# First 38 expert tiles of an attention-and-experts kernel as 19 pairs with standing weights

## The chip, the cores and the metric

The kernel runs on one core of a Trainium2 chip. The metric is the device time of one execution in microseconds (us); lower is better.

## The reference

A batch of 32 sequences of 112 tokens with 256 channels (x) and a context of 375 rows of 192 channels. Cut to what is computed:

```python
x = x + xattn(layernorm(x), ctx)          # 16 heads of 64, softmax over 375 keys, projection 1024 -> 256
h = layernorm(x)
p = softmax(h @ gate_w); take the best 2 of 8 experts, shares normalised to 1
gate, up = split(h @ gate_up_w[e])        # 256 -> 2 * 512
y_e = (silu(gate) * up) @ down_w[e]       # 512 -> 256
x = x + sum over the 2 experts of share * y_e
```

3584 tokens with two experts each make 7168 rows of expert work, in float32.

## The kernel before

**Stages.** First the attention, two batches to an iteration, up to about 1130 us. While it runs, each token's normalised row h, with its token number and share behind it (258 floats), is scattered twice into `bins`, an HBM buffer with one region for each expert. Then the experts' stage: rows are taken from the bins in tiles of 128 rows of one expert. There are always NT = 63 tiles. The first N1 = 45 are whole tiles that can be planned before the last two batches are in the bins; the plan for the rest (`tiles_left`, `experts_left`, `rows_left` on VectorE) is worked out beside the first tiles, along with the last two batches' routing. `tile_row` and `tile_expert` hold each tile's place and expert; engines read them into registers.

**Precision.** Each float32 product is made of three matmuls on a high and a low part of both operands (`split_product`: high x high, high x low, low x high). ScalarE writes high parts by a copy, VectorE low parts by a subtraction. All experts' gate and up weights stand in SBUF as both parts (`Wgu`, 4 KB a row), the down weights (`Wd`) whole, for all 8 experts; the parts of one tile's down weights are made anew for each tile in `down_even` / `down_odd`.

**A tile t.** SyncE (`load_rows`, L595) loads 128 rows into one of four slots of `h_in`. TensorE turns them (`turn_rows`, L1678, 2 transposes); ScalarE (L963) and VectorE (L1347) make `hT_h`, `hT_l`; VectorE keeps token numbers and shares (`keep_dest`, L1355, L1356). TensorE's gate and up products (`hidden`, L1692) have the 128 rows as standing weights and 512 expert columns moving: 6 matmuls of 512 columns each. ScalarE applies silu (L992), VectorE multiplies (L1390) into `silu` [128 rows, 512]. That lies the wrong way round for the down product, so TensorE turns it (L1729, 4 transposes), ScalarE and VectorE make `hidT_h` (L987) and `hidT_l` (L1382). The down product has 12 matmuls of 256 columns. ScalarE scales by the share (L1008, `y_out`, `y_done`); GpSimd adds the rows into `out` in HBM by an indirect accumulating transfer (L822, semaphores `y_store`). An addition is issued only when the one before it has landed, since two tiles may hold the same token.

**Order.** Each engine runs its own stream written by hand in `four_tiles` (three iterations unrolled, then a loop of 4 tiles). TensorE's order in iteration t is: turn rows of t+1, turn hidden of t-1, up product of t, gate product of t+1, down product of t-1. ScalarE's: rows' high part of t+1, hidden high part of t-1, silu of t, down weights' high part of t (L1000), output of t-1. VectorE's: rows' low part, hidden low part of t-1, `keep_dest` of t+1, multiply of t, down weights' low part of t (L1392). SyncE only loads rows, up to 3 tiles ahead. All matmuls of `split_product` stand under L1429, row transposes under L1682. Before the stage, experts' gate and up weights are loaded by SyncE and ScalarE (L443), split by ScalarE (L857) and VectorE (L1138), and `Wd` by two SyncE transfers of 1024 and 3072 KB during the last attention batches.

## Time and profile before

| | us |
|---|---|
| median of 3 runs | 1472.36 (1471.12 to 1476.83) |
| the profiled execution | 1469.35 |
| its span, first to last instruction | 1467.6 |
| TensorE busy | 1426.4 (97%) |
| VectorE / ScalarE / GpSimd busy | 1054.7 / 854.5 / 624.9 |
| mean granted TensorE clock | 0.994 |

All times inside the kernel are us from the start of that span. A releaser, as in "<-PE bank L1429", is the instruction whose semaphore ended a wait. TensorE's matmuls overlap in the records: the pace of a stream is read from the starts, not from the durations.

### The profile page before, as it was taken

How to read it: one execution, taken by the hardware profiler on the slowest of the kernel's cores; microseconds unless marked ns; L12 is line 12 of the kernel's file. 1: busy time of each engine (PE TensorE's matmuls, PEld its weight loads, DVE VectorE, ACT ScalarE, POOL GpSimd, SP SyncE). 2: the span in 40 equal slices, each digit the busy share in tenths (PEclk: the TensorE clock that was granted, in tenths of full speed). 3: DMA queues.
4: the chain of work that ended last, by engine and by line, in shares of the span. 5: the costliest groups of instructions: out<-in, count | busy, mean ns of one | idle time of the engine just before them, and what ended most of it. 6: DMA issues, size and time to landing. Idle time of an engine off the chain costs nothing.

```text
span 1467.6 us, 38599 instructions
## 1 busy us (share of the span) xinstructions
PE 1426.4 (97%) x11960; PEld 1264.4 (86%) x11961; DVE 1054.7 (72%) x2868; ACT 854.5 (58%) x2392; POOL 624.9 (43%) x671
## 2 busy tenths in 40 slices
PE   6999999999999999999999999999997999999996
PEld 5888889888888888888888898888886788888885
DVE  5667777777777777777777777777767776666664
ACT  5566556555665566656655656566555565555553
POOL 3634344344545343544344444545436243333332
PEclk9999999999999999999999999999999999999999
DMA  9322222222222232322222222212128243333232
GB/s 264 108 68 69 75 72 76 67 76 67 73 67 75 72 88 76 99 74 67 73 67 77 70 73 70 73 38 73 31 64 312 50 69 54 57 51 57 51 57 26
DMA packets 101508, 114.75 MB, mean 78 GB/s; under 512 B 17276, under 2 KB 88172, under 8 KB 101356
## 3 DMA queue, kind: packets, MB, share of 16 engines
q1 hardware_dynamic: 88300, 95.25, 22.3%
q0 software_dynamic: 12144, 15.66, 6.0%
q10 hardware_dynamic: 1024, 3.34, 0.7%
q8 instruction: 21, 0.34, 0.1%
q14 instruction: 19, 0.16, 0.0%
HBM read 62.28 MB, written 51.93 MB: 78 GB/s over the span
## 4 chain that ended last, share of the span: by engine, by line
PE 91%; DVE 3%; DMA 3%; issue 1%; ACT 0%; ACTq 0%; POOLq 0%; DVEq 0%; SPq 0%
PE bank L1486 26%; PE bank L1429 21%; PE bank L1555 11%; PE bank L1531 10%; PE bank L1521 9%; PE bank L1576 6%; PE bank L1493 4%; DMA out<-y_out,dest_now 2%; PE bank L1729 2%; DVE probT L1285 1%; PE bank L1682 1%; DVE Wgu L1138 1%; DMA WkU_whole<-in_L_xattn_Wkv 1%; DVE stat L1127 0%; DVE x L1125 0%
## 5 line engine op out<-in xcount | busy, mean ns | idle before, releaser
L891 ACT ACTIVATE prob<-bank,neg_max 112x375 f32<-112x375 f32 x512 | 300.4, 589 | 136.1 <-DVE neg_max L1279 136.1
L1279 DVE TENSOR_REDUCE neg_max<-bank 112x1 f32<-112x375 f32 x512 | 243.8, 539 | 16.4 <-PE bank L1521 16.3
L1531 PE MATMUL bank<-ident,prob 112*125 112x112 f32 x1536 | 213.8, 273 | 2.6 <-ACT prob L891 2.4
L1531 PEld LDWEIGHTS bank<-ident,prob 112*125 112x125 f32 x1536 | 198.3, 188 | 16.1 <-ACT prob L891 4.7
L1555 PEld LDWEIGHTS bank<-probT,V 125*64 125x64 f32 x3072 | 149.0, 137 | 39.7 <-issue 37.0
L822 POOL DMA_INDIRECT out<-y_out,dest_now x63 | 97.8, 1552 | 199.9 <-DMA out<-y_out,dest_now 139.8
L1046 DVE TENSOR_TENSOR K_l<-bank,K_h 128x376 fp32r<-128x376 f32 x256 | 140.3, 549 | 57.1 <-ACT K_h L847 52.7
L1555 PE MATMUL bank<-probT,V 125*64 125x112 f32 x3072 | 176.6, 264 | 3.3 <-DVE probT L1285 2.5
L1429 PE MATMUL bank<-Wgu,hT_h 128*128 x504 | 164.7, 408 | 3.4 <-DVE hT_l L1347 2.8
L845 ACT COPY V<-bank 125x512 f32<-125x512 f32 x96 | 56.4, 587 | 164.7 <-PE bank L1493 162.2
L847 ACT CAST K_h<-bank 128x376 fp32r<-128x376 f32 x256 | 121.0, 473 | 31.2 <-PE bank L1486 29.7
L745 POOL TENSOR_SCALAR std<-mv 112x1 f32<-112x1 f32 x32 | 7.7, 239 | 280.2 <-DVE mv L1132 280.2
L710 POOL CAST OT_h<-O_now 128x448 fp32r<-128x448 f32 x64 | 37.3, 583 | 210.0 <-DVE O_now L1115 210.0
L897 ACT COPY probT<-bank 125x336 f32<-125x336 f32 x256 | 101.7, 442 | 38.6 <-PE bank L1531 37.8
L1285 DVE COPY probT<-bank 125x336 f32<-125x336 f32 x256 | 123.8, 494 | 0.1
L1036 DVE COPY V<-bank 125x512 f32<-125x512 f32 x96 | 66.4, 691 | 78.1 <-PE bank L1493 75.1
L1486 PE MATMUL bank<-yA_h,WkH 128*128 128x376 f32 x256 | 99.6, 389 | 13.1 <-DVE WkU L1064 13.1
L1008 ACT ACTIVATE y_out<-bank,share_now 128x256 f32<-128x256 f32 x63 | 29.8, 474 | 137.5 <-PE bank L1429 137.5
L1429 PEld LDWEIGHTS bank<-Wgu,hT_h 128*128 128x128 f32 x504 | 89.7, 189 | 23.2 <-issue 6.6
L891 ACT ACTIVATION_READ_ACCUMULATOR prob<-bank,neg_max 112x1 f32 x512 | 108.3, 212 | 0.0
L1429 PE MATMUL bank<-Wgu,hT_l 128*128 x252 | 99.2, 394 | 0.0
L1486 PE MATMUL bank<-WvH,yA_h 128*125 128x512 f32 x192 | 91.0, 474 | 0.0
(217 smaller groups left out, 3962.1 us busy)
## 6 DMA issues: line engine op xcount, KB each, us to landing
bins<-pad_rows SPq DMA_DIRECT2D x29, 1032.0 KB, 6.0
inv_rows<-sums SPq DMA_DIRECT2D x126, 128.0 KB, 2.9
h_in<-bins SPq DMA_DIRECT2D x63, 129.0 KB, 2.2
Wgu<-in_L_ffn_gate_up_w SPq DMA_DIRECT2D x6, 1024.0 KB, 6.8
y_sb<-in_ctx SPq DMA_DIRECT2D x32, 187.5 KB, 2.7
y_sb<-in_ctx SPq DMA_DIRECT2D x62, 93.8 KB, 2.7
x_sb<-in_x SPq DMA_DIRECT2D x16, 224.0 KB, 2.9
x_res<-in_x SPq DMA_DIRECT2D x32, 112.0 KB, 2.5
```

The source lines that it names most:

```text
L822: pool.indirect_dma_start(out, bass.IndirectOffsetOnAxis(ap=dest_now[:, (k + 3) % 4:(k + 3) % 4 + 1], axis=0), y_out[:, (k + 1) % 2, :], N ...
L847: nc.scalar.copy(K_h[:, arg, :], src[:, 0:LKE]).then_inc(hi_done, 1)
L891: nc.scalar.activation(prob[:, j, :], S_ps[j][0:LQ, 0:LKV], ACT.Exp, bias=neg_max[:, j:j + 1], accum_out=row_sum[:, head // HB, head % HB: ...
L897: nc.scalar.copy(probT[:, j, :], S_ps[j][0:KR, 0:KT * LQ]).then_inc(probT_second, 1)
L1046: nc.vector.tensor_tensor(lo, ps, hi.bitcast(F32), ALU.subtract).then_inc(lo_done, 1)
L1279: nc.vector.tensor_reduce(neg_max[:, j:j + 1], S_ps[j][0:LQ, 0:LKV], AX.X, ALU.max, negate=True).then_inc(max_done, 1)
L1285: nc.vector.tensor_copy(probT[:, j, :], S_ps[j][0:KR, 0:KT * LQ]).then_inc(probT_first, 1)
L1429: last = mm(dst, w, m, start=n == 0, stop=n == len(todo) - 1)
L1486: last = mm(out, w, y, start=begins and n == 0, stop=ends and n == "both")
L1521: last = mm(S_ps[2 * k + r][0:LQ, 0:LKE], w[rows, p, q], m[rows, p, :], start=n == 0, stop=n == len(todo) - 1)
L1531: last = nc.tensor.transpose(S_ps[j][0:KR, t * LQ:t * LQ + LQ], prob[:, j, t * KR:t * KR + KR], ident[0:LQ, 0:LQ])
L1555: last = mm(O_ps[r * DK:r * DK + DK, c:c + LQ], V[:, t, (2 * p + r) * DK:(2 * p + r) * DK + DK], probT[:, 2 * k + r, t * LQ:t * LQ + LQ], ...
```

## The change

- The first 38 tiles (N1 = 2 x 19) are planned as 19 pairs of one expert (PAIRS): 256 rows. 25 tiles remain single (before: 45 and 18).
- In a pair, 128 x 128 blocks of the expert's gate and up weights are the standing operand and the 256 turned rows move (`turned_hidden`): 12 matmuls of 256 columns for gate and as many for up, for each of two halves of the 512 hidden columns. The hidden values come out turned, and the pair has no transposes of them.
- These weights are held in `still`, one buffer for each half of gate and up, refilled for every pair: the high part by a copy on ScalarE (`hold_still`, 128 x 512 elements, four a pair), the low part by a transfer from `Wgu` to `still` inside SBUF (256 KB, four a pair, issued by SyncE, each behind the wait for the product that read the buffer last). The first pair's first half comes with both parts by transfer.
- `still` takes the place of most of `Wd`. `Wd` now has 2 slots; a pair's or single tile's down weights (512 KB) are loaded from HBM by SyncE (`load_down`, semaphores `wd_in`), two pairs or two tiles ahead. ScalarE waits for them in `hi_of_down`.
- In single tiles SyncE first waits for the addition of tile t-1, then loads rows of t+4 and down weights of t+2. The product of silu and up is written into `in_fours`, every fourth hidden column together, so that the down weights can be read with 4 KB in a piece.
- GpSimd issues a pair's two additions without a wait between them; before the first it waits for both of the pair before.
- The unrolled last-batch work and the plan move to pairs 0 to 7. The plan has one step more.
- TensorE's order in an iteration of pair p: down product of p-1, turn rows of p+1, gate and up of p's second half, gate and up of p+1's first half.

The core of the diff:

```diff
-N1 = -(-(2 * LQ * (B - 2) - E * (P - 1)) // P)
+PAIRS = -(-(2 * LQ * (B - 2) - E * (2 * P - 1)) // (2 * P))
+N1 = 2 * PAIRS
...
+def over_tiles(eng, pair_of_tiles, tile, end=PAIRS // 2, last=NT // 4):
+    for i in range(4):
+        for m in range(2):
+            pair_of_tiles(i, m)
+    with eng.Fori(4, end) as i:
+        for m in range(2):
+            pair_of_tiles(i, m)
...
+    pair_of_tiles(PAIRS // 2, 0)
+    for k in (2, 3):
+        tile(PAIRS // 2, k)
+    with eng.Fori(PAIRS // 2 + 1, last) as i:
+        for k in range(4):
+            tile(i, k)
...
+        place["at"] = wd_at
+        Wd = sb("Wd", [P, 2, FJ, C], F32)
+        still_at = place["at"]
...
+        in_fours = nc.alloc_sbuf_tensor_at("in_fours", [P, FJ, P], F32, offset=still_at)
...
+        still = sb("still", [P, 2, 2, 2, 2, 2 * P], F32R)
+        down_parts = [down_even, sb("down_odd", [P, 2, FJ, C], F32R)]
...
-                    sp.dma_start(Wd[:, 0:early].rearrange("p e k n -> p (e k) n"),
...
-                        sp.dma_start(Wd[:, early:E].rearrange("p e k n -> p (e k) n"),
...
+            def load_down(e, slot, rows="(k p)"):
+                sp.dma_start(Wd[:, slot], down_w[bass.ds(e, 1)].rearrange(f"o {rows} n -> p (o k) n", p=P)).then_inc(wd_in[slot], 16)
...
+            def hold_still(e, half, up, parts=slice(1, 2)):
+                first = up * FF + half * 2 * P
+                sp.dma_start(still[:, half, up, parts].bitcast(F32),
+                             Wgu[:, e, parts, :, first:first + 2 * P].bitcast(F32)).then_inc(still_in[half][up], 16)
...
+                sp.wait_ge(hT_made, t + 2)
+                sp.wait_ge(dest_done, t + 2)
+                sp.sem_inc(passed, 1)
+                for r in range(2):
+                    load_rows(t + 4 + r, 2 * m + r)
+                sp.wait_ge(wd_lo, p + 1)
+                sp.sem_inc(passed, 1)
+                if known(p) and p >= PAIRS - 2:
+                    load_down(expert_of(N1 + p - PAIRS + 2), m, "(p k)")
+                else:
+                    load_down(expert_of(t + 4), m)
+                for n, half in ((1, 1), (2, 0)):
+                    if there(p + n, PAIRS):
+                        e = expert_of(t + 2 * n)
+                        if known(p) and p + n == 1:
+                            sp.wait_ge(wgu_ready, e + 1)
+                            sp.sem_inc(passed, 1)
+                        if known(p) and p + n == 2:
+                            sp.wait_ge(wgu_ready, E)
+                        for up, made_it in enumerate((gate_made, up_made)):
+                            sp.wait_ge(made_it, 2 * p + n + 1)
+                            sp.sem_inc(passed, 1)
+                            hold_still(e, half, up)
...
+            def tile(i, k):
+                t = 4 * i + k
+                if there(t + 2, NT):
+                    sp.wait_ge(y_store[(k + 1) % 2], 16 * (2 * i + (k - 1) // 2 + 1))
+                    sp.sem_inc(passed, 1)
+                if there(t + 4, NT):
+                    sp.wait_ge(hT_made, t + 1)
+                    sp.wait_ge(dest_done, t + 1)
+                    sp.sem_inc(passed, 1)
+                    load_rows(t + 4, k)
+                if there(t + 2, NT):
+                    sp.wait_ge(wd_lo, t + 1 - PAIRS)
+                    sp.sem_inc(passed, 1)
+                    load_down(expert_of(t + 2), (k + 1) % 2, "(p k)")
+            for t in range(4):
+                load_rows(t, t)
+            first = expert_of(0)
+            sp.wait_ge(wgu_ready, first + 1)
+            sp.sem_inc(passed, 1)
+            for up in range(2):
+                hold_still(first, 0, up, slice(0, 2))
+            for up in range(2):
+                hold_still(first, 1, up)
+            for p in range(2):
+                load_down(expert_of(2 * p), p)
+            second = expert_of(2)
+            sp.wait_ge(wgu_ready, second + 1)
+            sp.sem_inc(passed, 1)
+            for up, made_it in enumerate((gate_made, up_made)):
+                sp.wait_ge(made_it, 1)
+                hold_still(second, 0, up)
+            over_tiles(sp, pair_of_tiles, tile, PAIRS // 2 - 1, NT // 4 - 1)
...
+            def hi_of_down(slot, landed):
+                act.wait_ge(wd_in[slot], 16 * landed)
+                nc.scalar.copy(down_parts[slot][:, 0], Wd[:, slot]).then_inc(wd_hi, 1)
...
+            def hold_still(e, half, up):
+                first = up * FF + half * 2 * P
+                nc.scalar.copy(still[:, half, up, 0], Wgu[:, e, 0, :, first:first + 2 * P].bitcast(F32)).then_inc(still_hi, 1)
+            def pair_of_tiles(i, m):
+                p, t = 2 * i + m, 4 * i + 2 * m
+                if there(p + 1, PAIRS):
+                    e = expert_of(t + 2)
+                    act.wait_ge(up_made, t + 1)
+                    hold_still(e, 0, 1)
+                if there(p - 1, PAIRS):
+                    for r in range(2):
+                        output(t - 2 + r, (2 * m + 2 + r) % 4, pair_down[r], 2 * i + m - 1)
+                if there(p + 1, PAIRS):
+                    hi_of_pair(p + 1, m)
+                else:
+                    hi_of_rows(N1, 0)
+                hi_of_hidden(p, 0)
+                silu_of_pair(p, 1)
+                if there(p + 1, PAIRS):
+                    hold_still(e, 1, 0)
+                    if not known(p) or p >= 1:
                         act.wait_ge(down_made, t)
+                    hi_of_down(1 - m, i + m + 1)
+                hi_of_hidden(p, 1)
+                if there(p + 1, PAIRS):
+                    silu_of_pair(p + 1, 0)
+                    act.wait_ge(up_made, t + 2)
+                    hold_still(e, 1, 1)
+                if there(p + 2, PAIRS):
+                    e = expert_of(t + 4)
+                    act.wait_ge(gate_made, t + 3)
+                    hold_still(e, 0, 0)
...
+            def tile(i, k):
+                t = 4 * i + k
+                if there(t + 1, NT):
+                    hi_of_rows(t + 1, (k + 1) % 2)
+                if there(t - 1, NT) and not (known(t) and t == N1):
+                    act.wait_ge(hidT_made, t - N1)
+                    act.wait_ge(down_made, t - 1)
+                    nc.scalar.copy(hidT_h[:].rearrange("p j n -> p (j n)"), hidT_ps[:]).then_inc(hidT_hi, 1)
+                if there(t, NT):
...
+                    act.wait_ge(down_made, t - 2 if known(t) and t == N1 else t - 1)
+                    hi_of_down((k + 1) % 2, 2 * i + (k - PAIRS) // 2 + 1)
+                if known(t) and t == N1:
+                    for r in range(2):
+                        output(t - 2 + r, (k + 2 + r) % 4, pair_down[r], PAIRS - 1)
+                elif there(t - 1, NT):
+                    output(t - 1, (k + 3) % 4, down_ps, 2 * i + (k - 1) // 2)
...
+            def pair_of_tiles(i, m):
+                p, t = 2 * i + m, 4 * i + 2 * m
+                for r in range(2):
+                    keep_dest(t + r, 2 * i + m - 1, 2 * m + r)
+                if there(p + 1, PAIRS):
+                    lo_of_pair(p + 1, m)
+                else:
+                    lo_of_rows(N1, 0)
+                lo_of_hidden(p, 0)
+                multiply(p, 1)
+                lo_of_hidden(p, 1)
+                if there(p + 1, PAIRS):
+                    multiply(p + 1, 0)
+                    lo_of_down(p + 1, 1 - m)
+                else:
+                    keep_dest(N1, PAIRS - 1, 2)
...
+                    nc.vector.tensor_tensor(in_fours[:].rearrange("p j n -> p n j"),
+                                            up_ps[k % 2][:].rearrange("p (n j) -> p n j", j=FJ),
+                                            silu[:].rearrange("p (n j) -> p n j", j=FJ), ALU.mult).then_inc(hid_done, 1)
+                    lo_of_down(t - PAIRS, (k + 1) % 2)
...
+            def turned_hidden(bank, half, up, slot):
+                w = still[:, half, up]
+                for c in range(2):
+                    cols = slice(c * P, c * P + P)
+                    last = split_product(bank[:, c * 2 * P:(c + 1) * 2 * P],
+                                         [(w[:, 0, j, cols], w[:, 1, j, cols], pairT_h[slot][:, j, :], pairT_l[slot][:, j, :])
+                                          for j in range(2)])
+                return last
...
+            def pair_of_tiles(i, m):
+                p = 2 * i + m
+                if there(p - 1, PAIRS):
+                    down_of_pair(p - 1, 1 - m)
+                if there(p + 1, PAIRS):
+                    turn_pair(i + m, 2 - 2 * m)
+                else:
+                    turn_rows(i, N1, 2)
+                gate_up(p, 1 - m, 1)
+                if there(p + 1, PAIRS):
+                    gate_up(p + 1, m, 0)
```

## Rows read from the trace of the kernel before

**Rows 1.** Table by stages: us, busy of each engine, PEclk, DMA share, GB/s.

```profile
1115.00:1133.00 18.00, 13.41 (x121) 11.45 (x119) 12.93 (x36) 8.65 (x20) 8.35 (x9) 0.91 1.00 345
1240.00:1440.00 200.00, 200.00 (x1230) 177.72 (x1229) 126.69 (x246) 108.95 (x205) 63.46 (x41) 1.00 0.31 53
```

**Rows 2.** Chain that ended last: start us, length us, what.

```profile
1206.27 4.23 PE bank L1429 x24
...
1435.86 4.25 PE bank L1429 x24
```

**Rows 3.** Timeline of TensorE in one tile: start us, length us, what.

```profile
1303.15 0.38 PE L1682 MATMUL bank<-ident,h_in 128*128 128x128 f32 x2
1303.37 0.60 PE L1729 MATMUL bank<-ident,silu 128*128 128x128 f32 x4
1303.73 0.71 PE L1429 MATMUL bank<-Wgu,hT_h 128*128 x2
...
1306.60 0.40 PE L1429 MATMUL bank<-down_odd,hidT_h 128*128 128x256 f32 x2
```

**Rows 4.** Timeline of ScalarE in one tile.

```profile
1303.50 0.47 ACT L1008 ACTIVATE y_out<-bank,share_now 128x256 f32<-128x256 f32 x1 [2.36 <-PE bank L1429]
...
1304.12 0.60 ACT L987 CAST hidT_h<-bank 128x512 fp32r<-128x512 f32 x1
...
1305.08 1.07 ACT L1000 CAST down_even<-Wd 128x1024 fp32r x1
```

**Rows 5.** Timeline of VectorE in one tile.

```profile
1305.48 0.69 DVE L1390 TENSOR_TENSOR silu<-bank,silu 128x512 f32<-128x512 f32 x1
1307.00 1.23 DVE L1392 TENSOR_TENSOR down_even<-Wd,down_even 128x1024 fp32r<-128x1024 f32 x1 [0.83 <-ACT down_even L1000]
```

**Rows 6.** Timelines, VectorE and TensorE at the stage's start, TensorE at iteration 60.

```profile
1131.42 10.38 DVE L1138 TENSOR_TENSOR Wgu<-Wgu 128x2048 fp32r<-128x2048 f32 x4
...
1142.38 0.72 PE L1429 MATMUL bank<-Wgu,hT_h 128*128 x2 [1.45 <-DVE hT_l L1347]
...
1439.93 0.38 PE L1682 MATMUL bank<-ident,h_in 128*128 128x128 f32 x2
```

**Rows 7.** Timeline of SyncE's queue, row loads one behind another.

```profile
1131.96 3.73 SPq L598 DMA_DIRECT2D h_in<-bins  x4
...
1155.16 0.34 SPq L598 DMA_DIRECT2D h_in<-bins  x1
...
1156.33 0.34 SPq L598 DMA_DIRECT2D h_in<-bins  x1
```

**Rows 8.** Chain near the end, and GpSimd's last addition.

```profile
1442.48 3.64 DMA out<-y_out,dest_now
1446.12 0.02 issue
...
1447.00 3.68 DMA out<-y_out,dest_now
...
1460.74 1.55 POOL L822 DMA_INDIRECT out<-y_out,dest_now  x1 [3.06 <-DMA out<-y_out,dest_now]
```

**Rows 9.** Transfers from 1240 us on (KB, us to landing), then experts' loads, L443.

```profile
h_in<-bins SPq DMA_DIRECT2D x39, 129.0 KB, 2.2
out<-y_out,dest_now POOLq DMA_INDIRECT x41, 4.0
...
L443 ACTq DMA_DIRECT2D Wgu<-in_L_ffn_gate_up_w x2: 419/464/509, 1129.5 to 1130.0; - x2
...
DMA to landing us min/median/max: 5.1/7.1/9.9
```

**Rows 10.** DMA queues from 1240 to 1440 us: packets, MB, share of 16 engines.

```profile
q0 software_dynamic: 5895, 5.37, 19.1%
q1 hardware_dynamic: 5625, 5.16, 12.2%
```

More of the change, by code:

```diff
@@ L184, in over_pairs @@
         body(NP)
-def over_tiles(eng, body):
-    body(0)
-    body(1)
-    body(2)
-    with eng.Fori(3, NT // 4) as i:
-        body(i)
-    body(NT // 4)
+def over_tiles(eng, pair_of_tiles, tile, end=PAIRS // 2, last=NT // 4):
[5 more added lines that the diff above has]
+            pair_of_tiles(i, m)
+    for i in range(end, PAIRS // 2):
+        for m in range(2):
+            pair_of_tiles(i, m)
+    pair_of_tiles(PAIRS // 2, 0)
[4 more added lines that the diff above has]
+            tile(i, k)
+    for i in range(last, NT // 4 + 1):
+        for k in range(4):
+            tile(i, k)
 def by_vector(b):
@@ L422, in attention_and_experts @@
         plan, scaled = sem("plan"), sem("scaled")
-        wd_early, wd_in = sem("wd_early"), sem("wd_in")
+        wd_in = [sem("wd_in0"), sem("wd_in1")]
+        still_in = [[sem(f"still_{n}{half}") for n in ("gate", "up")] for half in range(2)]
+        still_hi = sem("still_hi")
         wgu_raw = [sem(f"wgu_raw{e}") for e in range(E)]
@@ L830, in _, with add_rows, add_pair @@
-            over_tiles(pool, four_tiles)
+            def add_rows(slot):
+                pool.sem_inc(passed, 1)
+                pool.indirect_dma_start(
+                    out, bass.IndirectOffsetOnAxis(ap=dest_now[:, slot:slot + 1], axis=0),
+                    y_out[:, slot % 2, :], None, compute_op=ALU.add).then_inc(y_store[slot % 2], 16)
+            def add_pair(p, m):
+                for r in range(2):
+                    pool.wait_ge(y_done, 2 * p + r + 1)
+                    pool.wait_ge(dest_done, 2 * p + r + 1)
+                    if r == 0 and (not known(p) or p >= 1):
+                        for k in range(2):
+                            pool.wait_ge(y_store[k], 16 * p)
+                    add_rows(2 * m + r)
@@ L833, in _ @@
+            over_tiles(pool, pair_of_tiles, tile)
         @block.scalar
@@ L959, in _, with hi_of_pair, half_of_silu @@
                 load_expert(act, e)
+            def hi_of_pair(p, slot):
+                act.wait_ge(hT_made, 2 * p + 2)
+                nc.scalar.copy(pairT_h[slot][:].rearrange("p k n -> p (k n)"), hT_ps[:]).then_inc(hT_hi, 1)
+            open_gates(B - 2, A_ps[1])
+            hi_of_experts(4, 7)
+            hi_of_pair(0, 1)
+            hi_of_experts(7, E)
+            nc.scalar.activation(table[:], ident[:, 0:1], ACT.Silu)
+            def half_of_silu(half):
+                return silu[:] if half == 0 else hid_whole[:, 2:4, :].rearrange("p j n -> p (j n)")
@@ L1015, in _ @@
+            act.wait_ge(proj_made, B)
+            act.wait_ge(plan, N_PLAN1)
+            act.wait_ge(wgu_ready, 2)
+            e = expert_of(0)
+            for up in range(2):
+                hold_still(e, 1, up)
+            hi_of_down(0, 1)
+            silu_of_pair(0, 0)
+            e = expert_of(2)
+            hold_still(e, 0, 0)
+            over_tiles(act, pair_of_tiles, tile)
         @block.vector
@@ L1421, in _ @@
+            multiply(0, 0)
+            lo_of_down(0, 0)
+            over_tiles(dve, pair_of_tiles, tile)
         @block.tensor
```

430 lines of the change are left out of this document (227 added, 203 removed).

## The prediction, made before the result was known

> **What bounds the kernel now.** I read the table by stages first. From 1240 to 1440 us TensorE is busy for all 200.00 us at full clock and the DMA engines for 0.31 of it [rows 1]. The chain that ended last says the same: one piece of matmuls after another, from 1206.27 to 1435.86 us in 47 steps, 4.885 us a tile [rows 2]. TensorE's own timeline then splits a tile [rows 3]: 2 row transposes and 4 hidden transposes (1303.15 to 1303.73), 12 gate and up matmuls of 512 columns (to 1306.60, 2.87 us), 12 down matmuls of 256 columns (to 1308.04, by the tile's 4.885 us), so 0.36 us for the hidden transposes, 0.22 for the rows, 2.87 and 1.44. Only a part of TensorE's stream that goes away makes this stage shorter, and whatever holds its stream back makes it longer. The margins of what is hidden now decide the rest, so I read the other engines' timelines, the sync queue and the landings.
>
> **The part that gains: 19 pairs.** A pair needs 48 matmuls of 256 columns for gate and up. The 12 down matmuls show such a matmul with a weight load of its own at 0.12 us, half of the 0.239 us of 512 columns [rows 3], so a pair costs 5.74 us there, what two tiles cost now. The hidden values come out turned, so 8 transposes go: 0.72 us a pair. What is left is 5.74 + 2 x 1.44 + 0.44 = 9.05 us instead of 9.77. Bounds: 0 to 0.72 us a pair.
>
> Here a rule speaks against the change. The Trainium skill (TensorE: Matmul & The Clock Gate, "Back-to-back issue gap") gives a sustained spacing of about 81 ns for 128 columns and 131 ns for 512, so that halving the columns would not halve the time; drawn between its two figures, 24 matmuls of 256 columns would cost 0.8 us more a tile than 12 of 512, 30 us in all. The rows above disagree on both counts (239 ns for 512, half of it for 256), and the measurement decides.
>
> **Does anything else hold a pair back?** I count from the start of the previous pair's down product. ScalarE has 4 copies of standing weights of 512 columns, 2 silus, 3 high parts of 512, one of the down weights (1.07) and 2 outputs (0.47) [rows 4]: at 0.5 us a piece of 512 some 6.5 us of 9.05, with two register loads near 8. The tightest chain is up product (6.2) to VectorE's multiply (0.69), ScalarE's copy (0.60), VectorE's low part (0.69) [rows 4, 5]: ready at 8.3 to 8.4, wanted at 9.05. SyncE now reads 5 registers and issues 7 transfers a pair; a register load with its transfer takes 1.17 us [rows 7], so it is through in 7 us, and the low part most urgently wanted (gate, second half) leaves at 7.2 and is wanted at 12.35. I size its landing between the 2.2 us of 129 KB and the 5.1 of 1024 KB [rows 9]: 2.5 to 3.5 for 256 KB, no row shows a transfer inside SBUF. Bytes: 4 x 256 KB of low parts, 512 KB of down weights, 4 x 129 KB of rows in and out, about 2.1 MB in 9.05 us, 232 GB/s, where the engines moved 345 GB/s when full, with the 3 MB of Wd, in rows of 1 KB, among it [rows 1]. So pairs stay bound by TensorE; contention can cost 0 to 1.1 us a pair (below).
>
> **The opening.** The first gate product waits for VectorE's row of expert low parts (1131.42 to 1141.8) and starts at 1142.38 [rows 6]; both stay. Then the first pair wants 1.5 MB of standing weights and, behind them, 1 MB of down weights, where the kernel now has loaded all of Wd before: SyncE is free for them after 4 row loads from 1131.96 on, at 1136.6 [rows 7]; they share the DMA engines with the last experts, issued by 1130.0 and landed 9.9 later [rows 9], and at 345 GB/s land by 1147. ScalarE's copy of down weights stands ahead of the first silu, so about 1148.1 for it, then silu, rows, multiply, high and low parts: the first pair's down product at 1155.4 (13.0 us after the gate product; bounds 9.05 for the matmuls alone and 17). 17 pairs at 9.05 are 153.9. The last batch's routing and plan, now put behind pairs 0 to 7 on VectorE, costs 3 us (0 to 6). The last pair's remainder is 2.88 + 0.22 + 2.87 = 5.97, and the step to the singles (3 products of 1.44, 0.22, the pair's down product 2.87) 7.4. Sum: 1142.4 + 13.0 + 153.9 + 3 + 6.0 + 7.4 = 1325.7 us for the start of iteration 39. Now iteration 60 starts at 1439.93 [rows 6], so iteration 39 at 1439.93 - 21 x 4.885 = 1337.3. **Gain up to there: 11.6 us.**
>
> **The part that loses: 25 single tiles.** Their TensorE work is the same 4.885 us. But Wd is no longer resident: each tile's down weights (512 KB) come from HBM, and SyncE's `tile` issues tile T's load in iteration T-2, behind a wait for the output addition of tile T-3 to have landed. Queued behind that wait on SyncE are the row loads too. ScalarE waits for the load in `hi_of_down(T)`, and behind that wait on ScalarE stand the output of tile T-1, the next rows' high part and the hidden high part. That closes a loop from the landing of addition T-3 to that of addition T-1:
> - SyncE: row load and down load, 2 x 1.17 = 2.3 us [rows 7].
> - The load of 512 KB: on the line between 129 KB in 2.2 and 1024 KB in 5.1 us [rows 9], 3.4 (ends 2.2 and 5.1).
> - ScalarE: the copy 1.07, less the overlap of about 0.1, then the output 0.47 [rows 4]: 1.5.
> - GpSimd, from released to started: 1447.00 - 1446.12 = 0.9 [rows 8].
> - The addition: 3.64 to 3.68 in the chain, 4.0 the median by issues [rows 8, 9]: 3.7.
> Together 11.8 us; the load's pieces meet an addition's in one of the two phases, for which I add 0.2: 12.0 us for two tiles, against 9.77 that TensorE needs. The loop sets the pace: 6.0 us a tile. Between the ends of the load alone it is 10.8 to 13.7.
>
> From the start of iteration 39: addition 37 lands 5.9 later (output 0.6, GpSimd 0.9 and 0.7 behind addition 36, 3.7), weights 40 are there 5.7 after that (11.6), then 11 turns of the loop to the weights of tile 62 (132), then to the end 14.0: high part, low part (1.23 [rows 5]), down product 1.44, output and a queued addition land at 10.6, and 3.2 to 3.4 pass from a last landing to the end of the span, as now (the last addition starts at 1460.74 [rows 8], 3.7, span 1467.6). Sum 157.6. Now it is 1467.6 - 1337.3 = 130.3. **Loss: 27.3 us.**
>
> **Sum.** 1325.7 + 157.6 = 1483.3 us of span, 15.7 more than the profiled 1467.6; with the 1.75 that lie around the span, 1485 against the profiled execution's 1469.35. That execution lies 3.0 under the median of the runs, 1472.36, so on the median's scale **1488 us**.
>
> **The rivals.**
> - *The loop stays hidden (faster).* If the down weights arrive before ScalarE asks, the singles keep 4.885 us and 1488 - 27.3 gives 1461. The turn from slower to faster is at a loop of 10.6 us (11 turns cost what the pairs gain), and below 9.77 it costs nothing. For it: the loop's landing at its short end and no overlap of my other terms, 10.8. Against: even a 129 KB load takes 2.2, and each other term is read from a row. Chance 0.2, of which 0.14 by over 0.5%.
> - *The DMA engines bind the pairs too.* In the steady stretch additions take 19.1% and row loads 12.2% of 16 engines for 41 and 39 transfers of 128 rows [rows 10], that is 14.9 and 10.0 engine-us each. By that price of a row load (78 ns a piece) 1536 pieces of low parts and down weights take 120, with two additions and two row loads 170 engine-us, 10.6 us of 16 engines against 9.05. Over 19 pairs up to 22 us on top: 1488 + 22 = 1510. At full load a piece took less than at idle prices (345 GB/s), which speaks against. Chance 0.15. The skill's 435 GB/s for transfers inside SBUF (DMA: Bandwidth & Descriptors, "436 vs ~360") would make it rarer still; no row here shows one.
> - *The pairs are not cheaper*, since each of their waits (weights in, weights copied, silu, multiply) comes just in time: the 0.72 us a pair is lost, 1488 + 14 = 1502. Against: slacks of 0.65 us and more. Chance 0.08.
> - *The forecast*: 0.57, its own range 1475 to 1507 by a loop of 10.9 to 13.7.
>
> **How the numbers follow.** About 0.5% (7.4 us) is what a measurement of this kernel can tell from no change: 1465 to 1480. Of the forecast's 0.57, 0.11 lies below 1480 (a loop under 11.3), with 0.06 of the first rival that makes 0.17 for the same; 0.14 faster; 0.69 slower. The range reaches down to a loop of 10 us and up to the DMA-bound case, and leaves out the 0.14 of the first rival and some 0.04 above: 1466 to 1510.
>
> **What would show it.** Matmuls of a pair at 0.12 us, a pair's period 9.05, iteration 39 at 1326: else the first part is wrong. In the singles TensorE idles 1.1 us a tile, ScalarE's longest wait is that for the Wd landing ahead of the down weights' high part, and the additions' landings pair up at about 12 us for two tiles. If the singles run at 4.885 us with that wait absent, the prediction is wrong in its main term; if pairs show TensorE waiting for a landing of `still`, the second rival holds.

## The result and the profile after

| | before | after |
|---|---|---|
| median of the runs beside each other | 1473.66 (1471.12 to 1476.83, 4 runs) | 1514.22 (1512.14 to 1514.87, 4 runs) |
| profiled execution / its span | 1469.35 / 1467.6 | 1513.76 / 1512.0 |
| first gate product | 1142.38 | 1145.35 |
| start of iteration 39 | 1337.3 | 1338.8 |
| iteration 39 to the end of the span | 130.3 | 173.2 |

The ratio is 1.0272, 95% interval 1.0247 to 1.0296: slower by 2.7%, where 1488 was predicted with a range to 1510. The direction was right, and the single tiles are where it is lost, but both halves came out dearer than the sum said. The table by stages of the changed kernel (us, busy of each engine, PEclk, DMA share, GB/s) answers to [rows 1]:

```profile
1180.00:1220.00 40.00, 36.42 (x294) 35.85 (x293) 21.84 (x67) 27.66 (x48) 14.93 (x10) 0.96 0.84 217
1220.00:1260.00 40.00, 38.18 (x311) 37.82 (x310) 23.09 (x55) 28.19 (x50) 15.49 (x10) 0.96 0.84 218
1260.00:1300.00 40.00, 39.86 (x339) 39.66 (x338) 21.41 (x47) 29.90 (x53) 13.50 (x8) 1.00 0.89 237
...
1380.00:1500.00 120.00, 96.80 (x534) 81.60 (x532) 58.20 (x106) 48.47 (x90) 27.87 (x18) 0.94 0.47 116
```

In the pairs TensorE is almost full, with holes of 3.6 and 1.8 us in two of the stretches; the DMA share went from 0.31 to 0.84 and 0.89, at the 217 to 237 GB/s that the prediction had counted as 232. In the singles TensorE does nothing for 23 of 120 us, and no engine is full, nor the DMA: something waits for something in turn. The chain that ended last names it (start us, length us, what), where [rows 2] had only matmuls:

```profile
1428.50 5.32 DMA out<-y_out,dest_now
...
1434.07 0.26 SPq L614
...
1434.78 0.34 SPq L616
1435.36 0.27 SPq L620
...
1436.09 3.99 DMA Wd<-in_L_ffn_down_w
...
1441.05 0.48 ACT y_out L1107
1441.59 0.53 issue
...
1442.35 5.30 DMA out<-y_out,dest_now
```

An addition lands, SyncE then reads two registers and issues rows (L616) and down weights, they land, ScalarE makes the high part and the output, GpSimd issues the next addition but one: 13.85 us to a turn, for two tiles. It is the loop of the prediction, term by term, one turn in 12.0 us there:

| term | predicted | this turn |
|---|---|---|
| addition | 3.7 | 5.32 |
| SyncE | 2.3 | 2.27 (1433.82 to 1436.09) |
| load of 512 KB | 3.4 + 0.2 | 3.99 |
| ScalarE | 1.5 | 1.45 (1440.08 to 1441.53) |
| GpSimd | 0.9 | 0.82 |

ScalarE's waits from 1380 to 1500 us say the same from the other side (us in total, times, longest):

```profile
ACT down_odd L1099 <- DMA Wd<-in_L_ffn_down_w: 35.9, 9, 5.4
ACT down_even L1099 <- DMA Wd<-in_L_ffn_down_w: 34.1, 9, 5.0
```

70 us in 18 waits, and behind each stand the output of the tile before and the next rows' high part. TensorE's waits from 1130 to 1340 us, the pairs with their opening:

```profile
PE bank L1643 <- DMA still<-Wgu: 5.9, 4, 2.2
PE bank L1643 <- DVE pairT_l L1523: 4.9, 3, 3.1
...
PE bank L1643 <- DVE hid_l L1569: 1.2, 2, 0.8
```

So low parts land late four times. The pairs' own price is what was predicted. From the pair timeline of TensorE (start us, length us, what), 4 row transposes and 48 products of 256 columns lie between these starts, 6.10 us:

```profile
1282.02 0.60 PE L1904 MATMUL bank<-ident,h_in 128*128 128x128 f32 x4
...
1288.12 0.40 PE L1643 MATMUL bank<-down_odd,hid_h 128*128 128x256 f32 x2
```

Less the 0.44 of the transposes that is 5.66 us, 0.118 a matmul (predicted 0.12), and the undisturbed pairs, counted from down product to down product, take 8.87 to 9.0 us (predicted 9.05). The other pairs take up to 13.17, and the mean of the 17 is 9.79. That is no less than the 9.77 that two tiles took before: as measured, the pairs together gained nothing, and iteration 39 starts 1.5 us later than before, not 11.6 earlier.

### The profile page after: what moved, and what is told of

It reads as the page before. It is cut to its first block and busy times, and to the rows that moved or that the text cites. A ratio compares the mean times of both kernels' runs of the same rounds, so it can differ in the third digit from the quotient of the medians.

```text
span 1512.0 us, 39106 instructions
## 1 busy us (share of the span) xinstructions
PE 1433.8 (95%) x12264; PEld 1281.2 (85%) x12265; DVE 1034.8 (68%) x2830; ACT 882.7 (58%) x2429; POOL 628.9 (42%) x671
## 5 line engine op out<-in xcount | busy, mean ns | idle before, releaser
L1454 DVE TENSOR_REDUCE neg_max<-bank 112x1 f32<-112x375 f32 x512 | 243.7, 538 | 14.5 <-PE bank L1735 14.4
L1643 PE MATMUL bank<-pairT_h,still 128*128 128x256 f32 x608 | 117.0, 290 | 11.3 <-DMA still<-Wgu 5.9
L1643 PEld LDWEIGHTS bank<-pairT_h,still 128*128 128x128 f32 x608 | 98.1, 195 | 13.8 <-DVE pairT_l L1523 5.7
L1643 PE MATMUL bank<-Wgu,hT_h 128*128 x200 | 67.6, 419 | 28.7 <-DVE hT_l L1529 25.8
L946 ACT CAST q_h<-bank 128x224 fp32r<-128x224 f32 x128 | 45.6, 356 | 73.9 <-PE bank L1643 73.9
```

Source lines behind the costliest of these rows:

```text
L1454: nc.vector.tensor_reduce(neg_max[:, j:j + 1], S_ps[j][0:LQ, 0:LKV], AX.X, ALU.max, negate=True).then_inc(max_done, 1)
L1643: last = mm(dst, w, m, start=n == 0, stop=n == len(todo) - 1)
```

## The experiments

Four questions: is the loop of waits the whole loss of the singles (b, a, d); why is the addition in it 1.6 us longer than before (h, b, a); what holds up the pairs (n, r, q); and what is a version without these faults worth (s, t). Gaps between products are read from the starts in TensorE's timeline; a "pair gap" is from one pair's down product to the next, a "tile gap" from one tile's hidden transposes to the next. Ratios are to the kernel before on the same chip.

**b: no wait of SyncE for the addition, in singles.**

```diff
             def tile(i, k):
                 t = 4 * i + k
-                if there(t + 2, NT):
-                    sp.wait_ge(y_store[(k + 1) % 2], 16 * (2 * i + (k - 1) // 2 + 1))
-                    sp.sem_inc(passed, 1)
```

> The changed kernel, but in the single tiles SyncE no longer waits for the addition of tile t-1 before it loads rows and down weights. Loop theory (landing of an addition, load, ScalarE, output, next addition, 13.8 us for two tiles, sets the pace of the singles): the loop is cut at its start, loads are issued as soon as their slot is free, 2 us before ScalarE asks, and the singles fall from 6.84 us to between 4.9 and 5.3 a tile: 173 us from iteration 39 to the end become 131 to 140, the time 1473 to 1482. Contention theory (the 512 KB loads make each addition take 5.3 us instead of 3.7, and additions follow one another): 5.3 + 0.8 = 6.1 us a tile stays, about 1496.

1469.43 us, ratio 1.0006 (0.9982 to 1.0029): one wait made the difference between this change costing 2.7% and costing nothing. All tile gaps but the first two and the last two are 4.87 to 4.90 us, and from iteration 39 to the end it is 134.5 us (before 130.3). The ten runs lie in two groups, six at 1466.3 to 1470.7 and four at 1475.2 to 1478.2 us; no trace here shows what parts them. From 1380 to 1440 us, by stages:

```profile
1380.00:1440.00 60.00, 60.00 (x367) 53.22 (x366) 41.39 (x76) 33.42 (x62) 19.43 (x13) 1.00 0.66 162
```

TensorE is full while the DMA engines move more than in the changed kernel (162 against 116 GB/s). That the additions and the loads together are too much for them is refuted.

**a: ScalarE writes the output of t-1 before it takes the down weights of t.**

```diff
             def tile(i, k):
...
-                    hi_of_down((k + 1) % 2, 2 * i + (k - PAIRS) // 2 + 1)
...
                 elif there(t - 1, NT):
                     output(t - 1, (k + 3) % 4, down_ps, 2 * i + (k - 1) // 2)
+                if there(t, NT):
+                    hi_of_down((k + 1) % 2, 2 * i + (k - PAIRS) // 2 + 1)
```

> The changed kernel, but in the single tiles ScalarE writes the output of tile t-1 before it waits for the down weights of tile t (the two change places); SyncE's wait stays. Loop theory: the loop no longer goes through that place, it now spans three tiles: SyncE 2.3, load 4.0, high part 1.05, low part 1.23, the next rows' low part 0.4, gate and down product 2.9, output 0.6, GpSimd 0.8, addition 4.7: 18 us for three tiles, 6.0 a tile, some 17 us less than the changed kernel: 1497. Contention theory: additions at 5.3 + 0.8 give 6.1 us a tile, 1498, so this run alone does not tell them apart; if the order on ScalarE does not matter, 1514.

1504.79 us, ratio 1.0223 (1.0204 to 1.0243), 6.45 us for most tiles: less was won than expected. In the profiled execution, the slowest of the four (1510.79), the time from iteration 39 to the end is 172.5 us against 173.2, since the first two tile gaps (6.51 and 6.08 against 4.98 and 4.95) and the last (5.09 against 3.81) are longer; so the profile does not show where the median's 9 us come from. The two-tile loop is opened, for the output no longer stands behind the load. But the output waits for the down product, so now the down weights' high part does too, and the chain that ended last shows a second ring of 6.3 us a tile through four engines:

```profile
1439.84 3.11 PE bank L1644 x18
...
1443.39 1.05 ACT down_odd L1099
...
1445.60 0.43 DVE hT_l L1530
...
1446.16 3.10 PE bank L1644 x18
```

Down product, output, high part, low part, and behind the low part on VectorE the next rows' low part, for which TensorE waits. In places the chain still goes through additions and a load, the loop over three tiles of the expectation: from 1457.30 to 1476.45 us through additions of 5.63 and 5.08 and a load of 4.63. A reordering cut one loop and left two longer ones.

**d: no down loads from tile 40 on**, with the wait kept.

```diff
-                    load_down(expert_of(t + 2), (k + 1) % 2, "(p k)")
...
-                    hi_of_down((k + 1) % 2, 2 * i + (k - PAIRS) // 2 + 1)
+                    if known(t) and t < N1 + 2:
+                        hi_of_down((k + 1) % 2, 2 * i + (k - PAIRS) // 2 + 1)
+                    else:
+                        nc.scalar.copy(down_parts[(k + 1) % 2][:, 0], Wd[:, (k + 1) % 2]).then_inc(wd_hi, 1)
```

> The changed kernel without the loads of down weights from single tile 40 on (each tile uses what stands in its slot; this leaves out part of the computation); SyncE still waits for the addition before it loads rows. Both theories: the singles run at TensorE's own 4.885 us a tile, 131 us from iteration 39 to the end, 42 us less than with the loads, and an addition lands after 3.7 us again. If the singles stay above 5.3 us, something else than the loads holds them (the strided write of the product, the wait ahead of the row loads).

One run, 1470.5 us, tile gaps of 4.885 but for the first (6.79). From iteration 39 to the end it is 131.4 us, in b 134.5, against 173.2 in the changed kernel and 130.3 before. Either cut, at the wait or at the load, gives the loop's loss back, as a closed loop must; what b still lacks are its first two gaps (s). The loss is neither's own time.

**h: half of the down weights in singles' loads.**

```diff
-                    load_down(expert_of(t + 2), (k + 1) % 2, "(p k)")
+                    if known(t) and t < N1 + 2:
+                        load_down(expert_of(t + 2), (k + 1) % 2, "(p k)")
+                    else:
+                        e = expert_of(t + 2)
+                        sp.dma_start(Wd[:, (k + 1) % 2, 0:2], ...[:, 0:2]).then_inc(wd_in[(k + 1) % 2], 16)
```

> The changed kernel with its wait, but from single tile 42 on only half of the down weights (256 KB instead of 512 KB) is loaded, so the down product of those tiles uses stale halves. Theory (loop of SyncE, load, ScalarE, GpSimd, addition, with the addition lengthened by the other phase's load beside it): load 2.6 to 3.0 instead of 3.9, addition 4.3 to 4.6 instead of 5.3, loop 11.5 to 12.0 instead of 13.7, so 5.75 to 6.0 us a tile and a time near 1492 to 1495. Rival (the addition's 5.3 us does not come from the load's bytes): addition stays 5.2 to 5.4, loop 12.7, 6.3 us a tile, time 1502.

One run, 1489.9 us, tile gaps of 5.9 on the mean. The transfers issued from 1380 to 1440 us (KB each, median us from issue to landing) in this kernel:

```profile
Wd<-in_L_ffn_down_w SPq DMA_DIRECT2D x10, 256.0 KB, 2.8
out<-y_out,dest_now POOLq DMA_INDIRECT x10, 4.4
```

in b:

```profile
Wd<-in_L_ffn_down_w SPq DMA_DIRECT2D x12, 512.0 KB, 3.5
out<-y_out,dest_now POOLq DMA_INDIRECT x13, 3.9
```

and in d:

```profile
h_in<-bins SPq DMA_DIRECT2D x13, 129.0 KB, 2.0
out<-y_out,dest_now POOLq DMA_INDIRECT x13, 3.8
```

The addition takes 4.9 us beside loads of 512 KB in the changed kernel (same view, 9 of them), 4.4 beside 256 KB, 3.8 with none. But in b, with all 512 KB, it takes 3.9. What differs is when it starts. GpSimd's issue and SyncE's (start us, length us, what) in the changed kernel, in the turn of the chain above:

```profile
1428.50 1.55 POOL L894 DMA_INDIRECT out<-y_out,dest_now  x1 [5.32 <-ACT y_out L1107]
...
1429.23 0.34 SPq L625 DMA_DIRECT2D Wd<-in_L_ffn_down_w  x1
```

and in b:

```profile
1403.30 0.34 SPq L625 DMA_DIRECT2D Wd<-in_L_ffn_down_w  x1
...
1404.61 1.55 POOL L891 DMA_INDIRECT out<-y_out,dest_now  x1 [3.51 <-DMA out<-y_out,dest_now]
```

GpSimd works on the addition for 1.55 us before its last piece is out. In the changed kernel the additions of these 60 us start between 1.4 us ahead of the nearest load's issue and 0.7 us behind it, six of the nine some 0.5 us or more ahead, so their pieces run beside the load; the wait ties the two together. In b eleven of thirteen start 1.1 to 1.5 us behind one, when much of the load's 3.5 us is over. The kernel a, whose loads are whole, has both cases:

```profile
1411.47 1.55 POOL L894 DMA_INDIRECT out<-y_out,dest_now  x1 [4.86 <-ACT y_out L1107]
...
1412.73 0.34 SPq L625 DMA_DIRECT2D Wd<-in_L_ffn_down_w  x1
...
1431.07 0.34 SPq L625 DMA_DIRECT2D Wd<-in_L_ffn_down_w  x1
...
1431.59 1.55 POOL L894 DMA_INDIRECT out<-y_out,dest_now  x1 [5.28 <-ACT y_out L1107]
```

The first of these additions takes 5.7 us to landing, the second 3.9. Of a's additions from 1345 to 1480 us, the eleven that start 0.6 to 1.3 us ahead of a load's issue take 5.1 to 5.7, the three that start 0.3 to 0.8 behind one 3.9 to 4.5, and the two that start 1.6 and 1.9 ahead 3.7 and 4.0. In h the ten start 0.6 to 1.2 us ahead, and with half the bytes they take 4.0 to 4.7. So the load's bytes lengthen the addition, and by how much goes with the offset; no run changed the offset and nothing else.

**n: no low-part transfers after the first pair.**

```diff
                             sp.wait_ge(made_it, 2 * p + n + 1)
                             sp.sem_inc(passed, 1)
-                            hold_still(e, half, up)
...
-            for up, made_it in enumerate((gate_made, up_made)):
-                sp.wait_ge(made_it, 1)
-                hold_still(second, 0, up)
...
-                pe.wait_ge(still_in[half][up], 16 * (p + 1))
+                pe.wait_ge(still_in[half][up], 16)
```

> The changed kernel without the transfers of low parts inside SBUF after the first pair (later pairs use stale low parts; this leaves out part of the computation). Pairs took 166.5 us from the first to the nineteenth down product, against 17 x 9.0 = 153. Transfer theory (pairs wait for low parts that come late, at 1172, 1184, 1215 and 1235 us): the 13.5 us go but for at most 3, the down product of the last pair starts 10 to 13 us earlier. Routing theory (the last batches' routing and the plan on VectorE hold the pairs back, the transfers are late only with it): at most 3 us are gained. The singles stay at 6.84 us a tile in either case.

One run, 1498.57 us. The 18 pair gaps take 164.5 us instead of 177.0; the first 17 of them are 154.0, at 8.88 to 9.55 each, and the last one, the step to the singles, is 10.48 as in the changed kernel. By stages:

```profile
1220.00:1260.00 40.00, 40.00 (x342) 40.00 (x341) 23.60 (x55) 30.33 (x54) 14.42 (x10) 1.00 0.57 128
```

TensorE is full at a DMA share of 0.57 instead of 0.84. SyncE's waits and register loads are all still there, so the holes come from the transfers themselves.

**q: low parts of the second half issued before rows and down weights in pairs**, on top of b. The call for (1, 1) stands ahead of `load_rows`, the one for (2, 0) behind `load_down`.

> The kernel without the wait in singles (1469.4 us); in pairs SyncE issues the low parts of the second half before the row loads and the down load instead of after them. If the low parts land late because they are issued late (behind a wait and 1.2 us a register load with its transfer): stalls behind `still` mostly go, first to last down product from 174.7 to 164 to 167, time 1459 to 1462. If they are late because the transfers themselves take long beside the 512 KB load and the rows: the stalls stay in number, the row loads come later as well, time 1467 to 1473.

1469.71 us, ratio 0.9994 (0.9985 to 1.0004), and TensorE still waits 4.9 us in six places for `still`, against 7.6 in ten in b. The pair gaps take 173.5 us against 174.7 (the profiled execution, 1463.79, is the fastest of ten). So the order on SyncE is a small part of the cause at most. What is left is the landing itself, 3.6 us by the median here, at a DMA share of 0.83 from 1158 to 1325 us; that it is the company of 2.1 MB a pair that stretches the late ones is the reading that n and t allow and that the DMA shares just before such landings fit (below), not one tried by itself.

**r: low parts copied by GpSimd instead**, from the second pair on, on top of b.

```diff
+            def low_parts(p, n, half):
+                e = expert_of(2 * p + 2 * n)
+                for up, made_it in enumerate((gate_made, up_made)):
+                    first = up * FF + half * 2 * P
+                    pool.wait_ge(made_it, 2 * p + n + 1)
+                    pool.tensor_copy(still[:, half, up, 1], Wgu[:, e, 1, :, first:first + 2 * P].bitcast(F32)).then_inc(still_lo, 1)
...
+                for n, half in ((1, 1), (2, 0)):
+                    if there(p + n, PAIRS):
+                        low_parts(p, n, half)
```

> The kernel without the wait in singles (1469.4 us), and in the pairs from the second on every low part of standing weights is copied by GpSimd (four 128x512 copies a pair, some 0.66 us each by its 128x448 cast at 0.583) instead of by a transfer inside SBUF. Theory (the stalls inside pairs are low parts that land late, because transfers share SyncE's queue and the engines behind it): TensorE's stalls behind `still` go, a pair takes 8.9 to 9.1 us outside the routing pairs, first to last down product falls from 174.7 to some 164, the time to 1459. Rival (the pairs' surplus is TensorE's own spacing and waits for ScalarE, GpSimd's copies only add): no change within 3 us of 1469. Rival (GpSimd is late: additions and copies are one queue of 1.55 x 2 + 2.7 us a pair): stalls move to GpSimd, time at 1469 or above.

1467.7 us, ratio 0.9982 (0.9971 to 0.9994): less than expected, with 17 of 18 pair gaps at 8.96 to 10.5 and the first at 16.01. GpSimd's timeline (start us, length us, what, in brackets the idle time before it):

```profile
1160.10 2.45 POOL L816 TENSOR_SCALAR hn<-x,mv,std 112x256 f32<-112x256 f32 x2 [0.21 <-issue]
1162.51 2.27 POOL L904 CAST still<-Wgu 128x512 fp32r x4
```

TensorE's:

```profile
1163.16 0.58 PE L1647 MATMUL bank<-pairT_h,still 128*128 128x256 f32 x1 [4.16 <-POOL still L904]
```

and TensorE by steps of 2 us (us, PE busy, PEclk, DMA share, GB/s):

```profile
1164.00:1166.00 2.00, 2.00 (x11) 0.50 0.66 230
1166.00:1168.00 2.00, 2.00 (x11) 0.50 0.44 42
```

The copies had been put behind the last batch's normalisation, which waits for VectorE. TensorE stood for 4.16 us, and after that its granted clock was 0.50, the lower of its two levels, for some 6 us (the stretch from 1168 to 1170 has 0.74, the next 1.00): 11 matmuls in 2 us where the later rows have 19 or 20. The stall cost 4.2 us and then another 3.

**s: opening and switch mended**, on top of b: ScalarE's `hi_of_down(0, 1)` stands behind `silu_of_pair(0, 1)`, VectorE's `lo_of_down(0, 0)` likewise, and in singles `keep_dest` stands behind the multiply and the down weights' low part.

```diff
-                if there(t + 1, NT):
-                    keep_dest(t + 1, 2 * i + (k - 3) // 2 + 1, (k + 1) % 4)
                 if there(t, NT):
...
                     lo_of_down(t - PAIRS, (k + 1) % 2)
...
+                if there(t + 1, NT):
+                    keep_dest(t + 1, 2 * i + (k - 3) // 2 + 1, (k + 1) % 4)
```

> The kernel without the wait in singles (1469.4 us), with two places mended: ScalarE splits the first down weights after silu of the first two halves instead of before (it waited 1.82 us for that load with the high parts of the next pair behind it), and VectorE keeps a tile's destinations behind its multiply in singles (it waited 3.02 and 4.93 us there for additions at the switch from pairs). Theory: the opening gets 2 to 3 us shorter, the first two single gaps fall from 8.18 and 6.49 to near 4.9 (4.9 us less), time 1461 to 1463. Rival (what is next late at the switch, the additions of the last pairs themselves or the row loads, takes it back): time 1466 to 1470.

1465.81 us, ratio 0.9965 (0.9951 to 0.9979). What VectorE did in b, at the switch:

```profile
1332.83 0.15 DVE L1540 CAST dest_now<-h_in 128x1 int32<-128x1 f32 x1 [3.02 <-DMA out<-y_out,dest_now]
...
1341.48 0.15 DVE L1540 CAST dest_now<-h_in 128x1 int32<-128x1 f32 x1 [4.93 <-DMA out<-y_out,dest_now]
```

The first tile gaps are now 4.90 and 4.89 instead of 8.18 and 6.49, and from gate product to first down product it is 12.2 us instead of 14.5. That is 2.3 and 4.9 us, of which the median shows 3.6. The expected 1461 to 1463 was the sum of both; the measured time lies between it and the rival's 1466 to 1470, nearer the rival. At the switch the step from the last pair takes 11.3 us instead of 10.5, so about 0.9 us is taken back there, but not all, as the rival would have it; the rest of the difference is not placed.

**t: all of it**, with GpSimd's copies only from the third pair's low parts on.

> The three mends together: no wait of SyncE in singles, the opening and the switch as in the kernel with both ends mended (1465.8 us, of which the 18 gaps between the pairs' down products take 175.6), and GpSimd copies for the low parts, but only from the third pair's on, so that its copies no longer stand behind the last batch's normalisation (which cost a stall of 4.16 us and half the clock for some 6 us after it). Theory (transfers inside SBUF are the pairs' surplus): gaps of 8.95 to 9.1 outside the first two and the routing ones, 18 gaps in 165 to 167 us, time 1455 to 1458, ratio 0.990 to 0.992 to the kernel before. Rival (the gains overlap, since a pair that is late in one place was going to wait in another): 1462 to 1466.

1458.37 us, ratio 0.9935 (0.9911 to 0.9959): faster than the kernel before by 0.65%, and its runs lie further apart than the forecast of 1455 to 1458 had room for: seven at 1454.8 to 1459.0 and five at 1465.1 to 1470.2. The 18 pair gaps take 167.2 us; in the profiled execution (span 1456.1) one tile gap at the switch is 6.29 again. By stages, a stretch of pairs and the singles:

```profile
1220.00:1260.00 40.00, 39.45 (x332) 39.05 (x332) 25.13 (x55) 29.64 (x52) 27.59 (x27) 1.00 0.56 126
...
1325.00:1440.00 115.00, 113.84 (x700) 100.94 (x699) 77.98 (x138) 62.45 (x117) 37.01 (x24) 1.00 0.66 157
```

## Why the prediction was right or wrong

The span came out 28.7 us over the predicted 1483.3 (1512.0). By the steps of the sum:

| step | predicted | measured | off by |
|---|---|---|---|
| first gate product | 1142.4 | 1145.35 | +3.0 |
| opening, to the first down product | 13.0 | 13.6 | +0.6 |
| 17 pairs, with the routing | 153.9 + 3 | 166.5 | +9.6 |
| last pair's remainder and the step to singles | 13.4 | 13.3 | -0.1 |
| iteration 39 to the end | 157.6 | 173.2 | +15.6 |

- **What bounds the kernel; the pair's price.** Right for a pair that nothing disturbs: 0.118 us a matmul of 256 columns, pairs of 8.87 to 9.05, and n, r and t run whole stretches at it. By an estimate drawn between the figures of the Trainium skill (TensorE: Matmul & The Clock Gate, "Back-to-back issue gap"), 81 ns for 128 and 131 ns for 512 columns, pairs would have been dearer than two tiles; the trace after gives 118 ns for 256 columns, half of the 239 for 512 [rows 3], and the measurement decides. Of the rival that pairs are not cheaper, the outcome came all the same, a mean pair of 9.79 us against 9.77, by one of the waits that it names, the weights in (5.9 us, with the clock behind it); the others cost 1.2 us in all.
- **The first gate product: "both stay".** It lay between 1139.7 and 1145.4 in the profiled executions of the changed kernel and the nine others, whose attention part is the changed kernel's own. The 3.0 us are within what differs from one execution to the next, and no term of the change.
- **"Contention can cost 0 to 1.1 us a pair".** The step named the right cause and its range held the size (9.6 / 17 = 0.56), but the sum took it at nothing. That is the first mis-sized term. Part of it are waits, 5.9 us for `still` and 1.2 for `hid_l`; part is the clock, which the prediction had not priced. TensorE's row after the longest of these waits:

```profile
1184.68 0.40 PE L1643 MATMUL bank<-pairT_h,still 128*128 128x256 f32 x1 [2.18 <-DMA still<-Wgu]
```

and the table in steps of 2 us for TensorE alone (us, PE busy, PEclk, DMA share, GB/s):

```profile
1184.00:1186.00 2.00, 1.32 (x7) 0.73 0.83 257
1186.00:1188.00 2.00, 2.00 (x11) 0.50 0.91 139
1188.00:1190.00 2.00, 2.00 (x18) 0.92 0.88 162
```

  From 1184.68 to 1188.29 us the matmuls start 0.213 us apart instead of 0.118, which makes 1.6 us on top of the 2.18. The wait of 1.82 us at 1235.76 was followed by the same (clock 0.53 and 0.62 in the next two steps, 1.6 us), the waits of 1.23 and 0.64 us by none. That a landing late by a little can cost more than its lateness is what the prediction had no term for. Over 17 times the 8.97 us of an undisturbed pair, 152.5, the pairs took 14.0 us: waits of 5.9 and 1.2, 3.2 by the clock, and 2.4 to 3.4 for the routing, by what its pairs take over 8.97 in t; 0.3 to 1.3 us are not placed. In t, without the transfers, the same 17 gaps are 156.7 us, where the prediction's sum has 156.9.
- **The second rival, the DMA engines as the bound of the pairs.** As the bound of all pairs at 10.6 us it fell: the stretch with a share of 0.89 has hardly a hole. But the sign that the prediction gave for it, TensorE waiting for a landing of `still`, came four times, and the engines were full just then: in the 2 us before each of these waits ended their share was 1.00 to 1.12 at 297 to 383 GB/s, against 0.85 on the mean from 1160 to 1320 us. Before the longest (us, PE busy, PEclk, DMA share, GB/s):

```profile
1182.68:1184.68 2.00, 0.00 (x1) 1.00 1.09 383
```

  So the engines bind the pairs in bursts. The rival's price was also summed too low: 10.6 against 9.05 is 1.55 us a pair, over 19 pairs 29 us and not 22, and its end would have been 1517 and not 1510. That 1514 lies inside such a range would have been luck, for more than half of the excess came in the singles.
- **The landing of a low part, 2.5 to 3.5 us.** 3.6 in q. The bound was just too low, and it was a median that was sized, where the worst of four a pair decides.
- **The opening.** 13.6 against 13.0, but with a wait that the working did not see: ScalarE's high part of the down weights stands ahead of silu, waited 1.82 us, and TensorE then waited 3.05 for the next pair's rows, which stood behind it on ScalarE. In s and t, where the copy stands behind silu, the opening takes 12.2 and 12.8 us, in the changed kernel and the seven others 13.6 to 14.7.

```profile
1150.49 1.05 ACT L1099 CAST down_even<-Wd 128x1024 fp32r<-128x1024 f32 x1 [1.82 <-DMA Wd<-in_L_ffn_down_w]
```

- **The loop in the singles.** The mechanism, its five members and their order were right, and b and d confirm it by both cuts. The rival in which it stays hidden fell. The sizes: addition 3.7, measured 5.3; load 3.6 with the 0.2, measured 3.8 to 4.0; the other three within 0.1. A tile takes 6.84 us instead of 6.0, over 20 tiles 16.8 us, of which the start and the tail gave 1.2 back. The failed step is "the load's pieces meet an addition's in one of the two phases, for which I add 0.2". The two phases are half a turn apart, about 6.9 us, and each load leaves within 1.4 us of the other phase's addition, in every turn. The prices came from [rows 8, 9], where no large load ran beside an addition. The range for the loop, 10.8 to 13.7, moved the load alone to its end; with the addition at its measured 5.3 as well it would have ended at 15.3 us and the time at some 1524.
- **The range.** It ended at the 1510 of one rival. But the two kinds of contention add up: 9.6 in the pairs and 15.6 in the singles are both more bytes beside what was there, and the cases had been kept apart as if only one could come.

What stays open: why the runs of t (and those of b, less widely) lie in two groups, whether the offset alone spares the addition in b, and what decides whether the clock falls after a wait (below).

## What to carry to other kernels

A wait put on a queue has to be followed round until it closes: here SyncE's wait for an addition, a load behind it, a copy waiting for the load and an output behind the copy made a ring of 13.85 us, and cutting it at the wait or at the load gave 39 and 42 us back from iteration 39 on. The durations for such a ring must come from rows in which the same transfers run side by side, since the ring itself ties them together; where no row has that, the term's upper end belongs into the range together with that of its neighbours. An engine that has room (GpSimd) can be the better carrier for copies inside SBUF than a DMA queue that is already the busiest thing, if nothing slow stands ahead of them on it.

## What the runs showed of the hardware

- TensorE's granted clock after a wait within a full stream: the waits of 1.82, 2.18 and 4.16 us were followed by some 3.5, 3.6 and 6 us at half of it, those of 0.64 and 1.23 us by none. The length of the wait does not settle it: behind waits for `still` of 1.91 us in a (ended at 1184.11) and 1.98 us in h (1179.59), and behind one of 2.46 us in a single tile of the changed kernel (1353.38), the clock stayed at 1.00. The singles of the changed kernel, with a hole in every tile, show 0.94 on the mean.
- An accumulating transfer of 128 rows takes 3.8 us beside row loads alone (d), 4.4 beside loads of 256 KB (h), and beside 512 KB 3.7 to 5.7 by the offset between the two (a, b), 4.9 by the median and 5.3 in the ring of the changed kernel.
- VectorE's product written with a stride (every fourth column together) takes 1.07 us instead of the 0.69 of [rows 5]; in the singles it was hidden:

```profile
1450.27 1.08 DVE L1624 TENSOR_TENSOR in_fours<-bank,silu 128x512 f32<-128x512 f32 x1
```

- GpSimd's copies of 128 x 512 and VectorE slow each other. Four copies in a row took 2.27 us in r while VectorE did nothing (from 1162.51, shown above), three took 2.78 in t while VectorE worked:

```profile
1245.49 2.78 POOL L916 CAST still<-Wgu 128x512 fp32r x3
```

  VectorE's side, from 1180 to 1320 us, by line and form (count, busy us, mean ns), first in b, without such copies, then in t:

```profile
L1566 DVE TENSOR_TENSOR hid_l<-hid_whole,hid_h 128x512 fp32r<-128x512 f32 x15 | 10.4, 692 | 10.8 <-ACT hid_h L1086 10.8
...
L1587 DVE TENSOR_TENSOR hid_l<-hid_whole,hid_h 128x512 fp32r<-128x512 f32 x16 | 14.8, 924 | 11.6 <-ACT hid_h L1106 11.6
```

  This subtraction reads both operands from SBUF. The multiplies, which read one from a PSUM `bank`, keep their 690 to 692 ns in both kernels. The Trainium skill (Advanced Engine Details and Errata, "VectorE Performance Modes") says that VectorE's second SBUF port is shared with GpSimd, so that GpSimd's instructions and VectorE's two-port ones can block each other; the trace fits a shared port, but does not show which port an instruction uses.
